# Two narrow products in split form, intermediates in PSUM, and a new order of the input propagation

## What is computed

```python
x = _layernorm(x + L0(x, adj))   # hypergraph convolution, relu, layer norm, convolution, + x
x = _layernorm(x + L1(x, adj))   # relu([x, (adj @ x) / deg] @ W^T)
x = _layernorm(x + L2(x, adj))   # three times adj @ (x @ W) + b, relu behind the first two
x = _layernorm(x + L3(x, adj))   # relu((adj @ x) @ kernel)
```

## Time and profile before

| | |
|---|---|
| median of three runs | 1463.22 us (1462.11 to 1463.25) |
| profiled execution | 1463.48 us |
| its span, first to last instruction | 1461.7 us |
| granted TensorE clock over the span, share of full | 0.991 |
| busy: TensorE, VectorE, ScalarE, POOL | 1416.2, 1080.4, 1056.8, 851.7 us |
| moved by DMA | 47.04 MB, mean 32 GB/s |

### The profile page before, as it was taken

One profiled execution on the slowest core, in us unless ns is written; L12 is line 12 of the kernel. 1 busy time (PEld: TensorE's weight loads), 2 busy tenths in 40 slices (PEclk: granted clock), 3 DMA queues, 4 the chain that ended last, 5 costly groups with the idle time before them and its releaser, 6 DMA issues. The chain is left out here.

```text
span 1461.7 us, 33281 instructions
## 1 busy us (share of the span) xinstructions
PE 1416.2 (97%) x10896; PEld 1353.8 (93%) x10896; DVE 1080.4 (74%) x3744; ACT 1056.8 (72%) x2442; POOL 851.7 (58%) x776
## 2 busy tenths in 40 slices
PE   7899999999999999999999999999999999999974
PEld 6799999999999999999999999999999999999973
DVE  6667777777777777777777777777777777777663
ACT  4577777778777777777777777777777777777863
POOL 4565565565566566566566566566566566566542
PEclk9999999999999999999999999999999999999997
DMA  4001101101101101101101101101100100110000
GB/s 135 23 12 37 38 19 37 38 19 37 37 20 37 38 19 37 38 19 37 38 20 37 38 19 37 38 24 32 38 26 30 38 28 29 37 30 16 15 16 22
DMA packets 29946, 47.04 MB, mean 32 GB/s; under 512 B 3408, under 2 KB 12240, under 8 KB 29776
## 3 DMA queue, kind: packets, MB, share of 16 engines
q1 hardware_dynamic: 29776, 44.91, 9.8%
HBM read 28.12 MB, written 16.78 MB: 31 GB/s over the span
## 5 line engine op out<-in xcount | busy, mean ns | idle before, releaser
L1180 POOL TENSOR_TENSOR h_lo<-h_f,h_hi 128x512 fp32r<-128x512 f32 x128 | 166.2, 1298 | 373.4 <-ACT h_hi L541 373.4
L560 ACT ACTIVATE x<-n_s,n_shift,n_rstd 128x256 f32<-128x256 f32 x384 | 208.4, 590 | 101.0 <-DVE n_shift L832 101.0
L810 DVE BATCH_NORM_STATS2 n_st<-n_s 128x6 f32<-128x256 f32 x512 | 188.1, 409 | 7.6 <-POOL n_s L1254 5.2
L555 ACT ACTIVATE n_std<-n_mv,eps_c 128x2 f32<-128x2 f32 x256 | 74.7, 292 | 158.3 <-DVE n_mv L815 158.2
L1188 POOL TENSOR_TENSOR r_lo<-r_f,r_hi 128x512 fp32r<-128x512 f32 x128 | 163.5, 1299 | 36.6 <-ACT r_hi L541 36.4
L1246 POOL TENSOR_TENSOR n_s<-tk,mask 128x512 f32<-128x512 f32 x64 | 66.7, 1042 | 165.7 <-issue 150.4
L254 PE MATMUL psum<-v_hi,h_hi 128*128 128x256 f32 x512 | 148.9, 291 | 5.0 <-issue 5.0
L254 PE MATMUL psum<-A_f,x 128*128 128x128 f32 x1024 | 142.1, 282 | 5.4 <-ACT x L560 4.8
L254 PE MATMUL psum<-w2c_hi,r_hi 128*128 128x258 f32 x512 | 145.9, 285 | 0.5 <-POOL r_lo L1188 0.5
L254 PE MATMUL psum<-w2c_hi,r_lo 128*128 128x258 f32 x512 | 146.0, 285 | 0.0
L254 PE MATMUL psum<-w2c_lo,r_hi 128*128 128x258 f32 x512 | 144.8, 283 | 0.0
(11 more groups left out here) (141 smaller groups left out, 5044.1 us busy)
## 6 DMA issues: line engine op xcount, KB each, us to landing
x_in<-x_in_dram SPq DMA_DIRECT2D x64, 256.0 KB, 3.0
out<-x SPq DMA_DIRECT2D x64, 256.0 KB, 2.0
at_in<-adjT SPq DMA_DIRECT2D x64, 128.0 KB, 2.3
x<-v_in SPq DMA_DIRECT2D x3, 256.0 KB, 5.8
n_s<-w2T_in SPq DMA_DIRECT2D x2, 256.0 KB, 3.7
r_f<-w1T_in SPq DMA_DIRECT2D x2, 256.0 KB, 4.7
h_f<-wab_in SPq DMA_DIRECT2D x2, 256.0 KB, 6.0
rows<-rows_in SPq DMA_DIRECT2D x1, 256.0 KB, 6.1
```

The costliest lines, as they stand in the source:

```text
L555: act.activation(nm.std[:], nm.mv[:, :, 1], ACT.Sqrt, bias=eps_c[:, 0:1]).then_inc(nm.rooted, 1)
L560: last = act.activation(dst[:, g, :], nm.s[:, g, :], ACT.Identity, scale=nm.rstd[:, g:g + 1], bias=nm.shift[:, g:g + 1])
L810: last = dve.bn_stats(nm.st[:, g, :], nm.s[:, g, :])
L1180: return pool.tensor_tensor(dst[1][:], src, f(dst[0][:]), ALU.subtract).then_inc(signal, 1)
```

## The change

- **G** becomes fp32r. `BH` gets 258 columns: `HT` times the rounded inverse count, `HT` times the rest of it, and the weights' two halves. `HT` is 0 or 1 and needs no split. One product a graph, into two banks. ScalarE rounds (`round_weights`, `round_inverse`), POOL makes the rests and both halves of `BH`, VectorE adds the two results again (`dn` by a reduction, `Gl`, then `Gd` in two steps).
- **GP** becomes fp32r: `GT` and p_f are split (`round_GT`, `round_p` on ScalarE, `low_GT`, `low_p` on POOL), and each graph takes three products.
- **Intermediates in PSUM**: agg, n1's sum, the variance h_var, dn, and the moments of n2 and n3.
- **Order.** TensorE: Gx ahead of Ax3, H2 ahead of GP. ScalarE: h_mean, h_std and the GT copy ahead of n3's apply, Gx's split ahead of Ax3's, n2's and n1's roots earlier. VectorE: scale_G and the edges one after the other, n2's sum, statistics and moments ahead of the splits, Gx's split ahead of Ax3's. POOL: xb and the new low halves ahead of x2c.

The core of the diff:

```diff
-BANK = dict(R=0, Ax2=0, Tr=0, GP=0, H1=1, Gx=1, XAB=2, AXB=2, TK=2, H2=3, xT=4, P=4,
-            H2W=6, H1W=6, G=7, AP3=7, Ax3=7)
+BANK = dict(R=0, Ax2=0, Tr=0, GP=4, H1=1, Gx=1, XAB=2, AXB=2, TK=2, H2=3, xT=4, P=4,
+            H2W=6, H1W=6, G=(5, 7), AP3=7, Ax3=7)
...
-        n1, n2, n3, n4 = Norm("n1"), Norm("n2"), Norm("n3"), Norm("n4")
+        n1, n2 = Norm("n1", sums=False), Norm("n2", moments=BANK["H1W"])
+        n3, n4 = Norm("n3", moments=BANK["AP3"]), Norm("n4")
...
                 for g in range(2):
-                    last = mm(psum[:, BANK["G"], g * (C + 1):(g + 1) * (C + 1)], HT[:, g, :], BH[:, g, :],
-                              True, True)
+                    last = mm(psum[:, bank("G", p)[g], 0:2 * C + 2], HT[:, g, :], BH[:, g, :], True, True)
...
-                    if m == 2 and begun(n - 2) and not first(n, 2):
-                        pe.wait_ge(n1.summed, upto(n - 2))
+                    if m == 2 and begun(n - 4):
+                        pe.wait_ge(gt_hi, upto(n - 1))
...
+                if not first(n, 2):
+                    pe.wait_ge(gd_made, upto(n))
                 for h in range(2):
                     pe.wait_ge(r_lo[h], upto(p))
...
-                pe.wait_ge(p_made, upto(p))
-                if not first(n, 1):
-                    pe.wait_ge(gt_made, upto(n))
-                for g in range(2):
-                    last = mm(psum[:, bank("GP", p), g * D:(g + 1) * D], GT[(k - 1) % 2][:, g, :],
-                              p_f[:, g, :], True, True)
+                pe.wait_ge(p_hi, upto(p))
+                pe.wait_ge(p_lo, upto(p))
+                pe.wait_ge(gt_lo, upto(p))
+                for g in range(2):
+                    last = product(psum[:, bank("GP", p), g * D:(g + 1) * D],
+                                   [(part(GT_s[(k - 1) % 2], ALL, g), part(p_s, ALL, g))])
...
+            def round_GT(n, k):
...
+                copy(GT_s[k % 2][0][:].rearrange("p a b -> p (a b)"),
+                         psum[:, bank("Tr", p), 0:2 * C]).then_inc(gt_hi, 1)
+
+            def round_p(n, k):
...
+                copy(p_s[0][:], p_f[:]).then_inc(p_hi, 1)
...
                 if active("AP3", n):
                     p = n - 4
                     root(n3, p)
+                if active("P", n):
+                    square_mean(n, k)
+                    root_h(n, k)
+                if active("Tr", n):
+                    copy_GT(n, k)
+                if active("AP3", n):
+                    p = n - 4
                     if begun(p - 1):
                         act.wait_ge(pe_did["Ax3"], upto(p - 1))
                         act.wait_ge(n4.summed, upto(p - 1))
                         act.wait_ge(x3_nz, upto(p - 1))
                     apply(n3, p, x3)
-                if active("F", n):
-                    root(n4, n - 5)
-                if active("P", n):
-                    square_mean(n, k)
-                if active("Tr", n):
-                    copy_GT(n, k)
-                if active("P", n):
-                    root_h(n, k)
+                if active("GP", n):
+                    round_p(n, k)
...
-                dve.tensor_tensor(Gd[:], g_dn[:, :, 0:C], bc(dinv[:], [C, 2, C], 2), ALU.mult).then_inc(gd_made, 1)
+                dve.tensor_tensor(Gl[:], out_G(n, C, 2 * C), bc(dinv[:], [C, 2, C], 2), ALU.mult).then_inc(gl_made, 1)
+                dve.wait_ge(gl_made, upto(n))
+                for g in range(2):
+                    last = dve.scalar_tensor_tensor(out=Gd[:, g, :], in0=psum[:, bank("G", n)[g], 0:C],
+                                                    scalar=dinv[:, g:g + 1], in1=Gl[:, g, :],
+                                                    op0=ALU.mult, op1=ALU.add)
+                last.then_inc(gd_made, 1)
...
-                    last = dve.scalar_tensor_tensor(out=agg[:, g, :], in0=psum[:, BANK["AXB"] + g, 0:D],
+                    o = psum[:, BANK["AXB"] + g, 0:D]
+                    last = dve.scalar_tensor_tensor(out=o, in0=o,
                                                     scalar=rdeg[:, g:g + 1],
                                                     in1=xa[:, g, :], op0=ALU.mult, op1=ALU.add)
...
+            def low_p(n, k):
...
+                lo(p_s, p_f[:], p_lo)
+
+            def low_GT(n, k):
...
+                lo(GT_s[k % 2], GT[k % 2][:], gt_lo)
```

More of the change, by code:

```diff
@@ L78, in build @@
         sq, sq2, sq1 = sb("sq", [KH, 2, C]), sb("sq2", [2, 2, C]), sb("sq1", [2, C])
-        h_mean2, h_var = sb("h_mean2", [2]), sb("h_var", [2])
+        h_mean2 = sb("h_mean2", [2])
         h_veps, h_std, h_rstd = sb("h_veps", [2]), sb("h_std", [2]), sb("h_rstd", [2])
-        p_f = sb("p_f", [2, D])
+        p_f, p_s = sb("p_f", [2, D]), hi_lo("p", [2, D])
         xb = sb("xb", [2, D])
@@ L132, in build @@
         pe_R0 = sem("pe_R0")
[L133 to L136, removed]
+        ht_made, ht_counted, be_max, be_made, be_hi, be_lo, bh_made = (
+            sem(s) for s in ("ht_made", "ht_counted", "be_max", "be_made", "be_hi", "be_lo", "bh_made"))
+        dn_0, dn_1, dn_2, dn_3, gl_made, gd_made = (sem(s) for s in ("dn_0", "dn_1", "dn_2", "dn_3", "gl_made", "gd_made"))
+        w_hi, w_lo, gt_made, gx_hi, gx_lo = (sem(s) for s in ("w_hi", "w_lo", "gt_made", "gx_hi", "gx_lo"))
         r_relu, r_hi = [sem(f"r_relu{j}") for j in range(2)], [sem(f"r_hi{j}") for j in range(2)]
@@ L141, in build @@
         deg_max, deg_inv = sem("deg_max"), sem("deg_inv")
-        p_made, xb_made = sem("p_made"), sem("xb_made")
+        p_made, p_hi, p_lo, xb_made = sem("p_made"), sem("p_hi"), sem("p_lo"), sem("xb_made")
+        gt_hi, gt_lo = sem("gt_hi"), sem("gt_lo")
         a_hi, a_lo, a_copied = sem("a_hi"), sem("a_lo"), sem("a_copied")
@@ L170, in bank @@
         def bank(stage, pair):
+            if stage == "G" and pair == 2:
+                return 6, 7
             if stage == "Tr" and pair in (1, 2):
-                return 3
+                return 3 * pair
             if stage == "GP" and pair == 0:
@@ L284, in G @@
                 pe.wait_ge(bh_made, upto(p))
-                pe.wait_ge(w_made, upto(p))
+                pe.wait_ge(w_lo, upto(p))
+                if begun(p - 2) and not first(n, 2):
+                    pe.wait_ge(p_made, upto(p - 2))
                 if begun(p - 5):
@@ L296, in Tr @@
                     pe.wait_ge(eye_loaded, 16)
-                if first(n, 2):
-                    pe.wait_ge(betaW_made, 1)
                 pe.wait_ge(gd_made, upto(p))
@@ L363, in xT @@
                 pe.wait_ge(n1.done, upto(p))
-                if not first(n, 2):
+                if first(n, 2):
+                    pe.wait_ge(betaW_made, 1)
+                else:
                     pe.wait_ge(p_made, upto(p))
@@ L470, in betaW_rows @@
                 pe.wait_ge(beta_made, KH)
+                pe.wait_ge(gt_hi, 2)
                 for m in range(KH):
@@ L677, in fill @@
                 root_h(1, 1)
+                round_p(1, 1)
+                round_weights(1, 1)
+                round_inverse(1, 1)
                 relu_r(2, 2, 0)
@@ L937, in make_p @@
                 if begun(p - 1):
-                    dve.wait_ge(pe_did["GP"], upto(p - 1))
+                    dve.wait_ge(p_hi, upto(p - 1))
+                    dve.wait_ge(p_lo, upto(p - 1))
                 for g in range(2):
@@ L968, in sum_n2, with moments_n2 @@
                     dve.wait_ge(n2.done, upto(p - 1))
-                dve.scalar_tensor_tensor(out=n2.s[:], in0=agg[:], scalar=0.0, in1=x1[:],
+                dve.scalar_tensor_tensor(out=n2.s[:], in0=psum[:, BANK["AXB"]:BANK["AXB"] + 2, 0:D], scalar=0.0, in1=x1[:],
                                          op0=ALU.max, op1=ALU.add).then_inc(n2.summed, 1)
+            def moments_n2(n, k):
+                if first(n, 2):
+                    dve.wait_ge(gt_hi, upto(n))
+                if begun(n - 3):
+                    dve.wait_ge(h1w_out, upto(n - 3))
+                dve.wait_ge(n2.stats, upto(n - 2))
+                dve.memset(wait_pad[:], 0.0)
+                mean_var(n2)
             def sum_n1(n, k):
```

224 lines of the change are left out of this document (127 added, 97 removed).

## The result

The changed kernel takes **1542.97 us** (median of four runs, 1541.68 to 1543.66) against 1462.99 for the kernel before (four runs): the ratio is **1.055**, 95% interval 1.053 to 1.057. The prediction was 1470 with a range of 1457 to 1542. Its direction was right; the time is just outside the range, and the case that came true is not the one that it took as likeliest but its second one, the blocked shift, which it had put at 23.05 us per body and 1536.

A forecast was written before the change was run, and what follows sets the result against it. TensorE bounded the kernel before, VectorE's queue ahead of TK after: 15.29 + 6.66 = 21.95 us a body, 0.11 longer; times 60 bodies, 6.6 on 1463.48 gives 1470, range 1457 to 1542.

The forecast's parts named there:

- the blocked shift: Rival: n4's two-element shift on VectorE waits for POOL's x2c; body 23.05 us, time 1536; chance 0.30.
- free: Likeliest case: n4's shift on VectorE does not wait for POOL's x2c; body 21.95 us, time 1470; chance 0.46.
- first tenth: Start of a POOL instruction, claimed not to need the shared port; read from sq2 taking 1.34 in place of 1.30.
- The chain through ScalarE and POOL: From p_f's start through p_hi, p_lo and GT_lo to x2c on POOL, put at 3.53 us.
- The terms of the sum: Steps from Tr's start to TK's second product, mostly VectorE's queue: 6.56 us, 6.66 with the allowance.
- The allowance of 0.10: Added to the Tr-to-TK path for sums written into PSUM and instructions gathering several semaphores; bounds -0.10 and +0.25.
- the late third norm: Rival: HT and the edge-count clamp miss POOL's port gaps, h_var slips about 0.6 us; time 1500; chance 0.05.
- Fill and drain: Start and end of the kernel, outside the full bodies: change taken as 0, within 4 us either way.
- TensorE's own stretch from Tr to TK: TensorE's work without waits between Tr and TK after the change, put at 5.99 us.
- The estimate of 0.065 a moved operand: VectorE's extra us per operand moved to PSUM; two on the path would add 0.13, body 22.08; left out.
- The rival on TensorE: Rival: TensorE stays the bound because ax3_lo comes 0.7 us earlier; body 21.28 us, time 1430; chance 0.15.
- the first stretch: From TK's second product to Tr, TensorE products back to back: 15.50 us, forecast 15.29 after G's saving of 0.21.

The follow-up runs named there:

- the kernel with the new fill: Changed kernel with ax_lo first, n1's sum and root earlier, and, in the fill, weights and inverse rounded ahead of h_mean: 1449.0 us, ratio 0.990.

## Why the prediction was right and wrong

**The step that failed: the choice between free and blocked.** The mechanism, the place, and what is queued behind it (gx_lo, ax_lo, TK) were all in the blocked case, and its body of 23.05 is the measured 23.03. Its price was put too high, though, 1.10 for the 0.93 that 1.09 is over an unhindered 0.16 (from x2c's end to gx_lo it had 0.22, where the trace has 0.11, 716.93 to 717.04); the path without the stall was longer by about as much (below), and the two errors cancelled. That the measured body lay where the case had it was luck to this extent. The case's 1536 became 1543, past the upper end of the range, by the fill and the drain (below), which no case had in its sum. The blocked case was given 0.30 and the free one 0.46, for two reasons, and both were bad.

The first was a row read the wrong way round. sq2's 1.34 while HT was on the port was taken to say that POOL leaves the port free in its first tenth. HT was there first: POOL's instruction ahead of sq2, in its timeline of the kernel before, is

```profile
708.67 2.55 POOL L1188 TENSOR_TENSOR r_lo<-r_f,r_hi 128x512 fp32r<-128x512 f32 x2 [0.41 <-ACT r_hi L541]
```

It ended at 711.22, HT at 711.37. HT takes 0.28 where POOL leaves it alone and took 0.57 here, so it had waited for r_lo, ran between it and sq2, and sq2 came second. The row prices POOL in the second place. Nothing in it was about VectorE there. A page not weighed in the prediction says as much: by the Trainium skill (SBUF — State Buffer, section "SBUF: two separate sides") the pair of ports that VectorE and GpSimd share is a lock; whichever starts first, a GpSimd instruction that reads SBUF or a VectorE one with two SBUF inputs, has it for the whole instruction, and the other blocks. The rows of the shift agree: 1.25 us for a request 0.06 behind x2c's start, 0.55 for one 0.75 behind it, each ending 0.02 to 0.03 after x2c.

The second was the closeness itself. The request was worked out at 3.57 to 3.62 after p_f's start and x2c at 3.53; the trace has 3.75 and 3.54. The chain through ScalarE and POOL was right within 0.01, the one through VectorE 0.13 to 0.18 short. With a passage decided by 0.04 us and every unpriced gap on VectorE's side making the request later, blocked was the safer half: not an even chance.

**The terms of the sum.** The run with x2c early shows the free path at 6.79 where the sum had 6.66. Against the rows of the kernel after: up to p_f 1.21 for 1.17; p_f 0.79 for 0.79; degm and rdeg 0.46 for 0.36, the one large miss (rdeg starts at 713.09, agg's pair, which takes rdeg as its scalars, 0.27 later, where I had put 0.18); agg 0.92 for 0.89; n2's sum 0.72 for 0.71; statistics 0.67 for 0.64; inverse 0.19 for 0.18. The allowance of 0.10 covered about half. So even with a free passage the time would have been 1490, not 1470: 0.19 us in each body more than forecast, and the fill. Of the 80 us, then, 52 are the stall; some 18 are the longer way through VectorE's queue, which that run still has (22.14 a body for 21.84), and about 10 are fill and drain.

One sum of a rival is wrong: the late third norm's 1500 leaves out the 0.11 of the free case, 60 x 0.71 make it 1506. Nothing else was worked out from it.

**Fill and drain** were put at 0 within 4; they were 5.5 and 3.4. The split of p stands in the fill's chain, where no other pair's work covers it, and 2 of the 5.5 are POOL's BH step ahead of it; where the rest comes from was not tried.

**What held.** The bound moved from TensorE to VectorE's queue, with TK waiting for ax_lo. h_var starts 0.24 behind the end of P's sums (710.54 + 0.50 to 711.28), so the third norm was not the late one. TensorE's own stretch from Tr to TK was put at 5.99; where it didn't wait it took 5.99 to 6.03. G takes 0.24, as put (700.27 to xT's start at 700.51 in the kernel with the new fill). Operands and results in PSUM cost VectorE 0.01 to 0.02 each: n2's sum 0.69 for 0.68, agg's pair 0.88 for 0.86. The estimate of 0.065 a moved operand, which the prediction worked out from the Trainium skill (VectorE: DVE Perf Modes, section on the TRN2 errata) and left out of its sum, is not in these rows; the measurement decides.

**The rival on TensorE** (1430) was not this kernel but three new orders away from it, VectorE's, ScalarE's and the fill's: with them the same instructions run in 1449. It is 21.53 a body, not 21.28; nearly all of the 0.25 is in the first stretch, between Ax2 and XAB, which starts 0.11 behind the end of x1T's split (702.66 + 0.69 to 703.46): the next engine to be late is ScalarE, whose half of that split comes behind R's four steps. On TensorE the rows show G 0.21 and GP 0.16 shorter in each body. The run with GP in fp32 shows that GP's part hardly reaches the time; no run undoes G's. What the change puts in front of TK decided.

## What to carry to other kernels

Where an instruction of a few elements stands in VectorE's queue ahead of something that TensorE needs, look at its inputs and at what POOL runs at that moment: with two inputs in SBUF it lasted as long as the POOL instruction that was on, up to 1.27 us for 0.16. Move it behind the urgent work, or move POOL's long instruction away; either brought back 50 of 80 us here. And when a forecast hangs on which of two engines comes first by 0.04 us, don't call it even: ask which chain has the unpriced gaps, and whether the row that says "no wait" shows the engine in question in second place.
